# Two small TensorE transposes change places in a windowed-attention step

## What is computed

```python
q, k, v = split(layernorm(x) @ qkv_w + qkv_b)           # 16 heads of 8
local   = softmax(mask(q @ k.T * scale)) @ v            # each token sees the 128 tokens before it
lattn   = softmax(mask(rq @ rk.T * lscale))             # 4 heads over 64 pooled "latents"
remote  = (lattn @ rv) @ rout_w + rout_b
gate    = sigmoid(local @ gl_w + remote_h @ gr_w)
mixed   = gate * local + (1 - gate) * remote_h
x       = x + layernorm(mixed @ out_w + out_b)
# then x = x + layernorm(ffn(layernorm(x)))
```

## Time and profile before

| | us |
|---|---|
| median of 3 runs | 612.89 (610.32 to 614.6) |
| the profiled execution: its time | 620.31 |
| the profiled execution: its span, first to last instruction | 618.6 |
| mean granted TensorE clock in it | 0.965 |
| TensorE matmuls busy, share of the span | 571.3, 92% |
| VectorE / ScalarE / GpSimd busy | 72% / 47% / 56% |

### The profile page before, as it was taken

The page is one execution under the profiler, slowest core; times in us unless marked ns, Lnnn a source line. Parts: engine busy times, 40 slices in busy tenths (PEclk is TensorE's granted clock), DMA queues, the critical chain, the costliest instruction groups (busy, mean ns, idle before and its releaser), DMA issues. The chain is left out here.

```text
span 618.6 us, 17277 instructions
## 1 busy us (share of the span) xinstructions
PE 571.3 (92%) x5504; PEld 390.2 (63%) x5509; DVE 448.0 (72%) x2031; ACT 290.6 (47%) x787; POOL 344.9 (56%) x749
## 2 busy tenths in 40 slices
PE   7898869979999999899999999987799999999992
PEld 3555336747777677577777777754367766776672
DVE  6884458838888888688888888885464767766646
ACT  1464305727676676567776767773132121212110
POOL 4664202637885878658888588898212242432251
PEclk9997979969999999899999999998999999999997
DMA  4586850633542454255433440000000000000001
GB/s 132 176 259 180 200 111 9 133 50 46 59 52 41 50 66 50 30 54 63 49 45 52 59 58 11 4 2 1 2 2 0 2 19 17 17 0 17 19 18 34
DMA packets 56590, 33.83 MB, mean 55 GB/s; under 512 B 5850, under 2 KB 55426, under 8 KB 56506
## 3 DMA queue, kind: packets, MB, share of 16 engines
q1 hardware_dynamic: 55450, 32.45, 29.0%
q10 hardware_dynamic: 1056, 0.35, 0.2%
HBM read 21.18 MB, written 11.27 MB: 52 GB/s over the span
## 5 line engine op out<-in xcount | busy, mean ns | idle before, releaser
L1036 DVE CUSTOM_DVE_ANT_0 added<-psS,maskq 128x256 bf16<-128x256 f32 x512 | 205.5, 412 | 61.1 <-PE psS L893 53.7
L1267 ACT ACTIVATE probs<-psST 128x512 f32<-128x512 f32 x256 | 154.0, 603 | 109.5 <-PE psST L914 108.3
L914 PE MATMUL psST<-qst,kst 98*128 98x128 bf16 x1024 | 101.7, 222 | 5.0 <-DMA qst<-mT 4.7
L914 PEld LDWEIGHTS psST<-qst,kst 98*128 98x128 bf16 x1024 | 79.1, 99 | 28.0 <-DMA qst<-mT 6.7
L893 PE MATMUL psS<-kst,qst 68*128 68x256 bf16 x448 | 88.6, 280 | 1.3 <-DVE rowmax L1036 0.8
L930 PE MATMUL psPV<-probs,vst 128*9 128x128 f32 x2048 | 82.2, 280 | 0.8 <-POOL probs L1182 0.4
L1179 POOL TENSOR_SCALAR_AFFINE_SELECT probs<-probs 128x256 f32<-128x256 f32 x140 | 57.9, 413 | 33.9 <-ACT probs L1267 33.7
L1700 ACT ACTIVATE hT<-fpsH 128x512 f32<-128x512 f32 x32 | 19.1, 598 | 121.6 <-PE fpsH L1444 121.6
L1182 POOL TENSOR_SCALAR_AFFINE_SELECT probs<-probs 128x256 f32<-128x256 f32 x140 | 57.4, 410 | 0.0
L893 PEld LDWEIGHTS psS<-kst,qst 68*128 68x128 bf16 x448 | 35.0, 102 | 33.7 <-issue 22.3
L1441 PE MATMUL fpsH<-xehi,w1hi 128*128 128x512 f32 x128 | 55.7, 435 | 0.0
(11 more groups left out here) (179 smaller groups left out, 1144.3 us busy)
## 6 DMA issues: line engine op xcount, KB each, us to landing
qst<-q_parts SPq DMA_DIRECT2D x96, 64.0 KB
kst<-k_parts SPq DMA_DIRECT2D x96, 64.0 KB
q_parts<-split SPq DMA_DIRECT2D x8, 384.0 KB, 2.7
k_parts<-split SPq DMA_DIRECT2D x8, 384.0 KB, 2.9
v_tok<-vt SPq DMA_DIRECT2D x8, 288.0 KB, 3.3
vst<-v_tok SPq DMA_DIRECT2D x16, 144.0 KB
X<-in_L_attn_x_dram SPq DMA_DIRECT2D x8, 256.0 KB, 3.0
out_dram<-res SPq DMA_DIRECT2D x8, 256.0 KB, 2.2
```

The lines of the kernel that those rows point to most:

```text
L914: last = nc.tensor.matmul(bank[:, a, side * P:(side + 1) * P], kst[0:KALL, h, ring(n - 1 + side)], qst[0:KALL, h, ring(n)], start=not mask ...
L1036: taken = nc.vector.tensor_tensor_reduce(added[:, h], psS[g % 2][:, a], mask[:], 1.0, NEG * 4, ALU.add, ALU.max, rowmax[:, n.mod(2), h:h + 1])
L1267: nc.scalar.activation(probs[:, g], psST[g % 2][:].rearrange("p a c -> p (a c)"), ACT.Exp, scale=SCALE).then_inc(s_exp.sem, 1)
```

## The change

In step s on TensorE, the transpose of the row maxima moves from visit 2 to visit 3, between `scores_t` and `values(s, 0)`. The transpose of the mixed heads moves from visit 3 to visit 4, between `scores_t` and the four transposes of the value sums. On ScalarE the copy of `psM` to `mT` moves from behind the exponential of visit 2 to behind that of visit 3. The number of instructions, their operands and their semaphores stay the same; SP's program is not touched.

```diff
-                    if g == 2 and (s + 1).live:
-                        n = s + 1
-                        pe.wait_ge(s_neg.sem, s_neg.after(n))
-                        pe.wait_ge(s_lpTc.sem, s_lpTc.after(s - 1))
-                        nc.tensor.transpose(psM, mparts[:, n.mod(2)].rearrange("p a h -> p (a h)"),
-                                            identb[:]).then_inc(s_mT.sem, 1)
                     if g == 2 and (s - 1).live:
                         n = s - 1
                         pe.wait_ge(s_lpTc.sem, s_lpTc.after(n))
...
+                    if g == 3 and (s + 1).live:
+                        n = s + 1
+                        pe.wait_ge(s_neg.sem, s_neg.after(n))
+                        pe.wait_ge(s_lpTc.sem, s_lpTc.after(s - 1))
+                        nc.tensor.transpose(psM, mparts[:, n.mod(2)].rearrange("p a h -> p (a h)"),
+                                            identb[:]).then_inc(s_mT.sem, 1)
                     if g == 3 and s.live:
                         values(s, 0)
-                    if g == 3 and (s - 2).live:
+                    if g == 4 and (s - 2).live:
                         n = s - 2
                         if not (s - 1).live:
                             keep_warm(nc, last_bank, filler, 15)
...
-                    if g == 2 and (s + 1).live:
+                    if g == 3 and (s + 1).live:
                         n = s + 1
                         act.wait_ge(s_mT.sem, s_mT.after(n))
```

## The result

| | before | changed | ratio (95% interval) |
|---|---|---|---|
| first comparison, median us | 613.66 (610.32 to 614.6) | 640.1 (629.35 to 650.38) | 1.033 (1.020 to 1.045) |
| again on another occasion (six runs) | 618.11 | 637.78 (633.19 to 653.82) | 1.036 (1.028 to 1.045) |
| profiled execution: time, span | 620.31, 618.6 | 650.38, 648.7 | |
| mean granted clock in it | 0.965 | 0.933 | |

The change makes the kernel 3.3% slower, some 20 to 26 us. The ratios are taken without the executions that lie over 1.5% above the fastest of their kernel, the medians with them, so the two medians of the first row by themselves would give 1.043. The executions of the changed kernel lie much further apart than those of the kernel before; the experiment with work in place of the waits comes back to it. The profiled one is the longest of the first four, and its attention began 4.5 us later.

The account below looks back on a forecast made before the run. It took the starts of TensorE's matmuls to set the steady pace. From the profiled 620.3: -5.9 distances, +18.5 and +2.0 waits for mT, +8.5 clock gave 643.4; on the median 636.0 us, own range 630 to 646, eight in ten 618 to 648.

Parts of the forecast that it names:

- Distances on TensorE: Starts of TensorE's matmuls in visits 2 to 4: shorter distances from both moved transposes, -5.9 us (-4.4 to -7.5).
- the toll behind line 914: TensorE, visit 3: about 0.32 us behind line 914, assumed paid once for line 965 and `values` together.
- rival 4: TensorE, visit 3: `values` still pays 0.32 behind line 965; 5 us more on each case; chance inside the others.
- Visit 2's 0.25: TensorE, visit 2: without the row maxima's transpose, line 972 starts 0.23 behind line 914 instead of 0.48; gives 0.25 us back.
- the mixed heads' 0.05: TensorE, visit 4: their transpose takes 0.11 beside four of its kind instead of 0.16 alone; 1.6 us in 32 steps.
- The wait of line 995 for the copy: TensorE, late visit 4: copy mT would end about 0.2 us ahead of the mixed heads' transpose; cost put at nothing.
- Waits for mT: TensorE, odd steps: mT, behind later loads in SP's queue, adds 18.5 us of waiting, plus 2.0 in step 3.
- The clock: TensorE behind gaps: five short falls of the granted clock at 1.7 us each, +8.5 us (0 to 15).
- case 5: TensorE's clock stays low for longer, as behind step 3: each fall about 6 us, 648 and more; chance 0.07.
- bound of 1.34 us: TensorE: behind a gap of 1.34 us the clock did not fall; gaps of 1.34 and less were not followed by falls.
- nine gaps of 1.6 to 3.0 us: TensorE's waits for mT as the prediction summed them; five of nine taken to be followed by a clock fall.
- The rival of the other sign: SP's queue: mT passes the loads' remainder, or loads go faster; only distances count, 607.0 us (605.4 to 608.5); chance 0.12.

Follow-up runs that it names:

- the experiment with work in place of the waits: Changed kernel with ten filler matmuls ahead of the wait for mT in visit 0 of odd steps 7 to 27: 635.57 us, ratio 1.028.
- eight fillers: Changed kernel with eight filler matmuls ahead of the wait for mT in odd steps 7 to 27: 629.36 us, beside 637.78 for the changed kernel.

## Why the prediction was right

It forecast 636.0 us and a slower kernel; 640.1 and 637.8 were measured. The mechanism was the one described. Term by term:

**Distances on TensorE** (-5.9 forecast). Direction right, size low: -8.8 by the medians of the two kernels with divided loads, -10.3 by their `attend`. The term that was mis-sized is the distance from line 965 to `values`, bounded by 0.06 and 0.16 and put at 0.11: it is 0.01. The lower bound came from two matmuls of full width; a transpose in 32 columns and value products in 9 columns start 0.01 apart here. `values` itself then runs 0.58 to the next group instead of 0.56 (186.86 to 187.42 in the kernel before), 0.59 in step 9, so the real price is 0.03 to 0.04. That the toll behind line 914 is paid once (the prediction's rival 4 doubted it) is confirmed. Visit 2's 0.25 and the mixed heads' 0.05 came as read. A term was left out: without line 965 ahead of it the latents' product also gives 0.05 back (0.64 to 0.59), which its 0.71 in the earlier trace rows against 0.66 in the earlier trace rows could have told. With it, 0.25 + 0.05 - 0.04 + 0.05 = 0.31 accounts for the 0.30 measured.

**The wait of line 995 for the copy, put at nothing.** Right in visit 4, in visit 3 it would have been 0.33 us in every step, as the kernel with the maxima's move alone showed.

**Waits for mT** (+20.5 forecast for steps 3 to 27). In the changed kernel's two profiles 22.6 and 18.8 us against 4.7 before, so +17.9 and +14.1. The chain (the copy is late by the length of visit 2, the loads start later, and the 8 KB stand behind them) held in each link: 16.0 us from the first load to the release, nine waits, one in step 3 and eight behind it. The sum came out high, in part at least because it ran each pair for itself. A stretch of low clock makes the even step longer, and the next wait shorter: step 13 took 13.9 us with the low clock from 240 on, step 14 took 13.2 us with the gap of 2.68 us and the low clock behind it, and step 15 did not wait for `mT` at all. What each of the two did for step 15 is not separated here.

**The clock** (+8.5 forecast). With eight fillers 8.0 to 8.4 us were recovered. The profiles show more: in the first one about 34 us at half speed from 240 on, where the kernel before had 3.4 us, of which some is given back by shorter waits. Five short falls of 1.7 us were forecast. Behind waits for `mT` five came, three short ones and two of about 10 us (a fourth short one follows the gap in step 14); in the second profile there were four, one short and three of 10 to 14 us. So the number was right, the length was not, and the prediction's case 5 was no rare case but part of the usual one. Its bound of 1.34 us, below which no fall was seen, did not hold either: one came behind a wait of 1.21 us. For the whole of `attend`, 17.9 of waits, -9.3 for 31 steps and 15 for the clock (half of the 30 us more at half speed, an estimate from above) make 23.6, and 22.5 were measured.

The prediction spoke of nine gaps of 1.6 to 3.0 us, three of them below 2.1. Its own list has ten, from 0.6 us on, and eight of them at 1.6 or more. The total does not hang on this, since five falls were taken either way.

**The total.** It came closer than its terms did, and that is in part luck: the gain of the distances was 3 us larger than forecast and the waits 3 to 6 us smaller, while the clock cost between nothing and 6.5 us more than forecast.

**The rival of the other sign** (the queue takes it up) fell: with `mT` behind undivided loads every kernel with a late copy and no fillers waited for 13 to 23 us. Its other half, a gain where only the distances count, turned out true in a case that the prediction didn't look for: with the loads divided over two steps the late copy costs nothing, and the change is a gain of about 9 us.

## What to carry to other kernels

Before a small instruction is moved to a cheaper place, follow its result out of the engine: here 0.3 us a step was gained on TensorE, and the price was 2 us in every second step that a queue had not to spare, because a small urgent transfer stood behind big patient ones. Divide the big loads so that none of them stands ahead of the urgent one for long. Where an idle time of two microseconds repeats, count the low clock behind it as a second cost, and expect the times to scatter.

## What the hardware did that I had not expected

- A bf16 transpose with a 32-column stationary tile ahead of f32 value products with 9-column tiles costs 0.03 to 0.04 us: 0.01 us between their starts, and 0.02 to 0.03 us on the value products. Between matmuls of 128 columns the same transpose cost 0.30 us: 0.25 us ahead of the next group and 0.05 us on it.
- The low clock behind gaps of 2 to 3 us lasted either about 3.5 us or 10 to 14 us, from the same kind of gap (2.37 us: about 10 us of it; 2.68 us: 3.5 us), and behind one of 2.74 us, at 218.33, the clock stayed up.
- An 8 KB transfer on a queue of its own took 7.9 us, from its issue to the matmul that waited for it, while 1 MB and the loads were under way on another queue. From step 7 on it came in time.
- ScalarE started its next instruction 0.72 us behind the start of a transfer's issue, so an issue on a computing engine has to be placed like any other instruction.
